# A gated scan kernel: the C rows repacked from DRAM, the gathered rows in another buffer, both outputs ahead of the softplus

## The chip, the cores and the metric

The kernel runs on one core of a Trainium2 chip. The metric is the device time of one execution in microseconds. Five engines are programmed by hand in one file: TensorE (PE in the profile), VectorE (DVE), ScalarE (ACT), GpSimd (POOL) and SyncE (SP), which here only issues transfers. Each has its own instruction stream; they meet only at semaphores. Nothing is scheduled by a tool: the order of an engine's work is the order of the calls in its block.

## What is computed

Sixteen images of 256 channels and 1024 tokens. Group norm and a small mixture of experts give a scale and a shift for each channel; what follows is the second layer:

```python
xz = silu(in_proj_w @ x + in_proj_b)           # 768 x 256
x_ssm, res, gate = split(xz, 3)
xf = silu(conv3(x_ssm, dw_w) + dw_b)           # over tokens, per channel
x_h = gather(xf, perm)                         # a permutation per head, 2 heads
dbc = dbc_w @ xf + dbc_b                       # per head: dt, B (8), C (8)
dt = softplus(dbc[0]); dt, B, C gathered by perm too
h_t = exp(dt_t * A) * h_(t-1) + dt_t * B_t * x_t ;  y_t = C_t . h_t + D * x_t
y = gather(y, inverse of perm)
out = x + silu(out_proj_w @ (y * silu(gate) + res) + out_proj_b)
```

## The kernel before

The work goes in eight **phases** of two images each (`PH`, `NB`). After a prologue (statistics, the ranks that make the permutation, the front half of phase 0) every engine's block calls `cycle(i, ...)` for phase 0, three times a loop of two phases (1 and 2, 3 and 4, 5 and 6), and for phase 7. A cycle does the scan of phase i and, between its parts, the front half (projection, convolution, rows) of phase i + 1.

The permutation goes through DRAM. TensorE turns tiles of `xf` into rows of tokens, ScalarE copies them to `stage` (`rows_out`), VectorE adds a bias, and GpSimd scatters them to `xt_scratch` with 16 indirect transfers (`scatter`, L389). Each row holds the x values of both images and, behind them, dt, B and C. When all have landed, SyncE loads the rows to `xp` in two transfers (`load_rows`, L288: the narrow dt, B, C part, then the wide x part), writes the C part back to `cd_scratch` (`store_c`, L293) and reads it from there into `crow` in 16 transfers that repeat the rows over partitions (`load_c`, L302). The way back is alike: SyncE stores results to `yt_scratch` (L315), and GpSimd gathers them with 8 indirect transfers for each head (`gather`, L401) into `big`; TensorE turns them back (`turn_back`, L1303), VectorE multiplies by the gate (`gated`, L1059).

In chunks of 16 tokens the scan is matrix work. In order: VectorE and ScalarE make the softplus of dt (`softplus`, L958 to L985); TensorE sums it (`segments`, L1214, into `sg`); ScalarE takes eight exponentials (`decays`, L547, into `big`); VectorE makes factors from them (`factors`, L1021 `bblk`); TensorE makes chunk sums (`chunk_sums`, L1230); VectorE scans them (`scans`, L995, semaphore `hs_ready`). GpSimd multiplies the decays by the C rows, 16 instructions for each head (`weigh`, L413, semaphore `w_ready`); VectorE turns these into a causal weight block (`token_weights`, L1038 to L1049, semaphores `m_step`, `mblk_ready`), and TensorE applies it (`results`, L1251 and L1261). GpSimd also scales the projection weights of each image into `wsc` (L358): `weights_x`, `weights_gate`, `weights_residual`. The last is awaited by TensorE's `residual` through `wr_ready`.

TensorE's plain products all stand at L1183: `project`, `gate` and `residual`; the output product is L1313. Their banks `pj0` to `pj3` are drained by ScalarE. Three points of order matter below:

```python
# TensorE, cycle of phase 7 only, ahead of results(i, 0)
if not more:
    residual(i, par, range(0, 4), g_all)      # waits for wr_ready
# ScalarE, end of a cycle
output(i, 0)
if more:
    softplus(i + 1)
output(i, 1)
```

Of the kernel before, what the change touches and what calls it, by code (L numbers as in the profile page):

```python
# [75 lines left out]
def build(nc, x_d, w1g_d, b1g_d, w2_d, b2_d, inw_d, inb_d, dww_d, dwb_d, dbcw_d, dbcb_d, alog_d,  # L76
          dpar_d, mob_d, outw_d, outb_d, const_d, out_d):
    with ExitStack() as ctx:
# [160 lines left out]
        def _(sp):  # L239
# [37 lines left out]

            def load_rows(i):


                sp.wait_ge(rows_scattered, 256 * (i + 1))
# [9 lines left out]
            def store_c(i):  # L291
                sp.wait_ge(dbc_rows_in, 16 * (i + 1))
                sp.dma_start(bass.AP(cd_d, 0, [[S * NB, P], [P * S * NB, H * NT], [1, S * NB]]),  # L293
                             v(xp, NB * (P + 1 + S), (ROW, H * NT), (1, S * NB))).then_inc(c_stored, 16)

            def load_c(i):

                sp.wait_ge(c_stored, 16 * (i + 1))
                run = L * S * NB
# [11 lines left out]
            def cycle(i, par, half, more):  # L311
# [5 lines left out]
                if not last_phase(i):  # L317
                    load_rows(i + 1)
                    store_c(i + 1)
                store_out(i, par, 0)  # L320
                if not last_phase(i):
                    load_c(i + 1)
# [6 lines left out]

            load_rows(0)  # L330
            store_c(0)
            load_c(0)
# [12 lines left out]
        def _(pool):  # L345
# [33 lines left out]
            def scatter(i, tiles):  # L379
                for nt in tiles:  # L380

                    hold(stage_ready, i * NT + nt + 1)
                    if nt == 0:

                        hold(dbc_rows_in, 16 * i)
                        hold(x_rows_in, 16 * i)
                    for h in range(H):
# [5 lines left out]
            def gather(i, h):  # L393
                hold(y_stored[h], 16 * (i + 1))
                if h == 0:

                    hold(mblk_ready, H * (i + 1))
                    hold(hs_ready, H * NB * S * (i + 1))
                for nt in range(NT):
                    k = h * NT + nt  # L400
                    pool.indirect_dma_start(  # L401
                        out=v(big, k * NB * P, (1, NB * P)), out_offset=None, in_=yt_d.ap()[0:(h + 1) * N],
# [16 lines left out]
            def first_tap(i, b):  # L419

                for ot in range(CT):
                    hold(a_drained, i * A_U + b * 4 + ot * 2 + 2)

                    hold(x_full, (i * NB + b) * NT)
                    nc.gpsimd.tensor_scalar(v(xf, ot * N, (1, N)), v(xs, ot * (N + 2), (1, N)), v(small, DWW + ot * 3, (1, 1)), 0.0,  # L425
                                            ALU.mult, ALU.add).then_inc(conv_step[ot], 1)

            def cycle(i, par, half):
                more = not last_phase(i)
                weigh(i, 0)  # L430
                if more:
# [31 lines left out]
        def _(act):  # L463
# [176 lines left out]
            def cycle(i, par, half):  # L640
# [38 lines left out]
                if more:  # L679
                    softplus(i + 1)  # L680
# [766 lines left out]
```

## Time and profile before

| | |
|---|---|
| median of 3 runs | 1151.54 us (1150.46 to 1155.68) |
| profiled execution, its own time | 1155.78 us |
| its span, first to last instruction | 1154.0 us |
| mean granted TensorE clock | 0.853 of 2.4 GHz |
| busy: PE, DVE, ACT, POOL | 850.5, 592.2, 574.9, 531.5 us |

Phase 0's segments begin at 153.7 us, the next ones at 279.4, 407.4, 529.7, 657.8, 787.1, 922.3 and 1049.5 us, so a phase takes 122 to 135 us. No engine is busy all the time. The timeline of one engine lists its instructions, merged where they repeat, with the idle time ahead of them in brackets and what ended it. "remote" there, and "another core or an unknown queue" in the chain, stand for a semaphore event that the profile can't put to an instruction or a transfer; the kernel has one core only. Most numbers below are from phase 4, which stands for 1, 2 and 6 too.

### The profile page before, as it was taken

To read this page: it belongs to the slowest core of one execution; us is meant where nothing else is said; L and a number is where in the kernel's file an instruction comes from. 1 tells how busy PE (TensorE), PEld (TensorE's weight loads), DVE (VectorE), ACT (ScalarE), POOL (GpSimd) and SP (SyncE) were. 2 spreads that over 40 slices of the span, in tenths; PEclk is the share of its full clock that TensorE was granted. 3 is DMA by queue.
4 is the path that set the end of the run, shared out by engine and by line. 5 is a ranking of instruction groups with operands and counts; after the bars stand their busy time and mean duration, and the time that the engine had idled before them with its cause. 6 is when DMAs were issued, how large, how long until landed. Compare 5 with 4: busy or idle time off the path is not lost.

```text
span 1154.0 us, 12950 instructions
## 1 busy us (share of the span) xinstructions
PE 850.5 (74%) x3988; PEld 540.1 (47%) x3988; DVE 592.2 (51%) x1104; ACT 574.9 (50%) x1078; POOL 531.5 (46%) x628
## 2 busy tenths in 40 slices
PE   2039765849984789768995999567984989659946
PEld 0025444624663447534672457334662448425633
DVE  6966138416860468234860587034850578135823
ACT  4824425428652485427552765326552575328541
POOL 0002519560957055642756186623757066723450
PEclk9558767979996799978995999878996899869977
DMA  8830291238524391358032761448024581447132
GB/s 338 329 129 1 77 160 42 89 105 169 136 80 134 105 217 37 115 159 195 31 112 94 179 150 56 134 127 189 32 82 137 145 172 42 141 133 145 39 98 85
DMA packets 112051, 142.54 MB, mean 124 GB/s; under 512 B 41705, under 2 KB 91122, under 8 KB 111986
## 3 DMA queue, kind: packets, MB, share of 16 engines
q1 hardware_dynamic: 99698, 105.91, 35.2%
q0 software_dynamic: 12288, 35.80, 9.5%
q8 instruction: 36, 0.59, 0.2%
q14 instruction: 29, 0.24, 0.1%
HBM read 88.07 MB, written 53.61 MB: 123 GB/s over the span
## 4 chain that ended last, share of the span: by engine, by line
PE 44%; issue 14%; another core or an unknown queue 13%; DMA 9%; DVE 8%; ACT 7%; SPq 3%; POOL 1%; POOLq 0%; ACTq 0%; DVEq 0%
PE pj L1183 17%; DMA xb<-in_x 6%; PE pj L1313 5%; PE pj L1251 4%; PE st L1230 4%; SPq L302 3%; PE tp L1206 3%; PE pj L1261 2%; PE tp L1204 2%; PE tp L1303 2%; ACT big L547 2%; DVE rs L771 1%; PE tp L1241 1%; PE tp L1242 1%
## 5 line engine op out<-in xcount | busy, mean ns | idle before, releaser
L1183 PE MATMUL pj<-xb,wsc 128*128 128x512 f32 x768 | 390.0, 654 | 19.2 <-DMA xb<-in_x 9.6
L413 POOL TENSOR_TENSOR big<-big,crow 128x128 f32<-128x128 f32 x256 | 194.0, 797 | 279.4 <-DMA crow<-cd_scratch 195.6
L1183 PEld LDWEIGHTS pj<-xb,wsc 128*128 128x128 f32 x768 | 151.6, 208 | 180.5 <-issue 172.2
L389 POOL DMA_INDIRECT xt_scratch<-stage,idx x128 | 125.1, 977 | 71.1 <-issue 36.0
L401 POOL DMA_INDIRECT big<-yt_scratch,idx x128 | 124.7, 975 | 65.9 <-issue 37.1
L358 POOL TENSOR_SCALAR wsc<-inw,pcur 128x256 f32<-128x256 f32 x96 | 70.2, 749 | 173.9 <-DVE pcur L916 87.8
L1303 PE MATMUL tp<-cst,big 128*128 128x128 f32 x256 | 48.1, 335 | 131.5 <-DVE gt L1059 65.7
L1059 DVE TENSOR_TENSOR gt<-tp,gt 128x512 f32<-128x512 f32 x64 | 42.3, 688 | 156.6 <-remote 94.0
L559 ACT COPY stage<-tp 128x256 f32<-128x256 f32 x128 | 47.8, 375 | 142.5 <-PE tp L1206 62.6
L1313 PE MATMUL pj<-gt,outw 128*128 128x512 f32 x256 | 112.3, 597 | 0.1
L1303 PEld LDWEIGHTS tp<-cst,big 128*128 128x128 f32 x256 | 36.0, 170 | 152.9 <-DVE gt L1059 69.9
L618 ACT ACTIVATE rs<-pj,pcur 128x512 f32<-128x512 f32 x56 | 36.5, 692 | 136.5 <-PE pj L1183 88.4
L941 DVE TENSOR_TENSOR stage<-stage,small 128x68 f32<-128x68 f32 x64 | 14.7, 230 | 173.4 <-ACT stage L560 107.6
L933 DVE SCALAR_TENSOR_TENSOR xf<-xs,small,xf 128x1024 f32<-128x1024 f32 x64 | 86.2, 1357 | 3.2 <-POOL xf L425 1.4
L1230 PE MATMUL st<-bblk,xp 128*128 128x64 f32 x512 | 68.3, 292 | 21.2 <-DVE bblk L1021 20.3
L1230 PEld LDWEIGHTS st<-bblk,xp 128*128 128x128 f32 x512 | 67.6, 210 | 34.7 <-issue 33.6
L1204 PE MATMUL tp<-cst,xf 128*128 128x128 f32 x256 | 57.1, 308 | 33.3 <-ACT stage L560 20.4
L995 DVE TENSOR_TENSOR_SCAN hs<-big,st 128x64 f32<-128x64 f32 x256 | 49.0, 265 | 63.4 <-PE st L1230 63.4
L1251 PE MATMUL pj<-xp,mblk 128*128 128x128 f32 x512 | 69.6, 280 | 14.6 <-DVE mblk L1049 14.6
L1313 PEld LDWEIGHTS pj<-gt,outw 128*128 128x128 f32 x256 | 48.4, 192 | 58.4 <-issue 58.0
L1206 PEld LDWEIGHTS tp<-dbcw,xf 128*128 128x128 f32 x512 | 73.8, 208 | 0.0
L547 ACT ACTIVATE big<-sg,small 128x400 f32<-128x400 f32 x128 | 63.9, 610 | 19.9 <-POOL big L413 17.2
(192 smaller groups left out, 1317.1 us busy)
## 6 DMA issues: line engine op xcount, KB each, us to landing
xb<-in_x SPq DMA_DIRECT2D x32, 1024.0 KB, 8.0
xp<-xt_scratch SPq DMA_DIRECT2D x8, 2048.0 KB, 9.8
crow<-cd_scratch SPq DMA_DIRECT2D x128, 128.0 KB, 7.9
yt_scratch<-rs SPq DMA_DIRECT2D x16, 1024.0 KB, 4.4
out<-xb SPq DMA_DIRECT2D x16, 1024.0 KB, 4.9
xp<-xt_scratch SPq DMA_DIRECT2D x8, 272.0 KB, 3.5
xt_scratch<-stage,idx POOLq DMA_INDIRECT x128
big<-yt_scratch,idx POOLq DMA_INDIRECT x128
```

The costliest lines, as they stand in the source:

```text
L389: pool.indirect_dma_start(out=xt_d.ap(), out_offset=bass.IndirectOffsetOnAxis(ap=idx[:, k:k + 1], axis=0), in_=v(stage, (nt * H + h) * ROW ...
L401: pool.indirect_dma_start(out=v(big, k * NB * P, (1, NB * P)), out_offset=None, in_=yt_d.ap()[0:(h + 1) * N], in_offset=bass.IndirectOffse ...
L413: last = nc.gpsimd.tensor_tensor(v(big, W_OFF + (s * Q + b * NT) * L, (L, NT), (1, L)), v(big, s * EEW + SEG + b * NT * L, (L, NT), (1, L) ...
L547: last = nc.scalar.activation(v(big, s * EEW, (1, EEW)), v(sg, 0, (1, EEW)), ACT.Exp, scale=v(small, ANEG + h * S + s, (1, 1)))
L933: nc.vector.scalar_tensor_tensor(dst, tap(k), wt(k), dst, ALU.mult, ALU.add).then_inc(conv_step[ot], 1)
L1183: last = nc.tensor.matmul(o[:, :], v(wsc, (b * CT + ct) * 2 * C + slot * C + ot * P, (1, P)), x_view(par, b, ct, nt * HALF, HALF), start=( ...
L1204: nc.tensor.transpose(v(o, ct * P, (1, P)), tile(ct), const("ident"))
L1206: last = nc.tensor.matmul(v(o, 2 * P, (1, H * K1)), tile(ct), v(dbcw, ct * H * K1, (1, H * K1)), start=(ct == 0), stop=(ct == CT - 1))
L1230: last = nc.tensor.matmul(v(st, g * CPT * S, (1, CPT * S)), x_rows(h, b, g), v(bblk, (b * NT + g) * CPT * S, (1, CPT * S)), start=True, st ...
L1251: nc.tensor.matmul(v(pj[2 * b + e], gp * P, (1, P)), v(mblk, (b * NT + g) * P, (1, P)), x_rows(h, b, g), start=(gp == 0), stop=False, skip ...
L1303: last = nc.tensor.transpose(v(o, e * P, (1, P)), v(big, (h * NT + nq * 4 + e) * NB * P + b * P, (1, P)), const("ident"))
L1313: last = nc.tensor.matmul(o[:, :], v(outw, h * C + ot * P, (1, P)), v(gt, (b * CT + h) * N + nt * HALF, (1, HALF)), start=(h == 0), stop=( ...
```

## The change

Six edits that go together:

- **C rows.** `store_c` reads the C part out of `xt_scratch` itself, DRAM to DRAM, ahead of the row load, instead of from `xp` behind it. It now waits for the scatter.
- **Gathered rows** go to `crow` instead of `big`. So `gather` waits for `w_ready` (both weighings of the phase done) instead of `mblk_ready` and `hs_ready`; `load_c` waits until all rows are turned back; `decays` of head 0 no longer waits for that.
- **GpSimd's order**: `weights_residual` behind the second weighing, the first gather ahead of `weights_gate` of the second image.
- **First tap** of the second image's convolution from GpSimd to VectorE.
- **ScalarE's order**: both outputs ahead of the softplus, whose table is loaded once (a set with exponential and logarithm) ahead of its wait; the second image's convolution output behind two more drains.
- **TensorE's order**: two gate products ahead of the wait for `r_ready`.

```diff
+            def store_c(i):
+                sp.wait_ge(rows_scattered, 256 * (i + 1))
+                sp.dma_start(bass.AP(cd_d, 0, [[S * NB, P], [P * S * NB, H * NT], [1, S * NB]]),
+                             bass.AP(xt_d, NB * (P + 1 + S), [[ROW, P], [P * ROW, H * NT], [1, S * NB]])).then_inc(c_stored, 16)
...
-            def load_c(i):
+            def load_c(i, turned):
                 sp.wait_ge(c_stored, 16 * (i + 1))
+                wait(sp, y_full, turned)
...
                 if not last_phase(i):
+                    store_c(i + 1)
                     load_rows(i + 1)
-                    store_c(i + 1)
                 store_out(i, par, 0)
                 if not last_phase(i):
-                    load_c(i + 1)
+                    load_c(i + 1, i * Y_U + Y_U)
...
-                    hold(mblk_ready, H * (i + 1))
-                    hold(hs_ready, H * NB * S * (i + 1))
+                    hold(w_ready, H * (i + 1))
...
-                        out=v(big, k * NB * P, (1, NB * P)), out_offset=None, in_=yt_d.ap()[0:(h + 1) * N],
+                        out=v(crow, k * NB * P, (1, NB * P)), out_offset=None, in_=yt_d.ap()[0:(h + 1) * N],
...
+                weigh(i, 1)
                 weights_residual(i, par)
-                weigh(i, 1)
                 if more:
                     weights_gate(i + 1, 1 - par, 0)
+                gather(i, 0)
+                if more:
                     weights_gate(i + 1, 1 - par, 1)
-                    first_tap(i + 1, 1)
-                gather(i, 0)
...
+                nc.scalar.preload_act_table_set("natural_log_exp_and_others")
                 act.wait_ge(sp_v, i * 9 + 1)
...
                 output(i, 0)
+                output(i, 1)
                 if more:
                     softplus(i + 1)
-                output(i, 1)
...
+                if not first(i):
+                    gate(i, par, range(0, 2), before_g)
                 pe.wait_ge(r_ready, i * 2 + 2)
                 segments(i, 0)
```

Three places show the order of instructions; a row names line, operation, what is written and read, and the semaphores waited for. First GpSimd in a phase inside the loop, from the second weighing to the first scatter, before:

```order
L413 TENSOR_TENSOR big<-big,crow 128x128 x15
L352 ISA
L358 TENSOR_SCALAR wsc<-inw,pcur 128x256 [waits a_full]
L358 TENSOR_SCALAR wsc<-inw,pcur 128x256
L352 REGISTER_ALU
L358 TENSOR_SCALAR wsc<-inw,pcur 128x256 [waits a_full]
L358 TENSOR_SCALAR wsc<-inw,pcur 128x256
L352 REGISTER_ALU
L352 ISA [waits a_drained]
L425 TENSOR_SCALAR xf<-xs,small 128x1024 [waits x_full]
L425 TENSOR_SCALAR xf<-xs,small 128x1024 [waits a_drained,x_full]
```

The first gather followed behind these, with waits for `y_stored0`, `mblk_ready` and `hs_ready`. The same place now:

```order
L413 TENSOR_TENSOR big<-big,crow 128x128 x15
L358 TENSOR_SCALAR wsc<-inw,pcur 128x256 [waits e_full]
L358 TENSOR_SCALAR wsc<-inw,pcur 128x256 x3
L352 ISA
L358 TENSOR_SCALAR wsc<-inw,pcur 128x256 [waits a_full]
L358 TENSOR_SCALAR wsc<-inw,pcur 128x256
L352 REGISTER_ALU
L352 REGISTER_ALU [waits y_stored0]
L401 DMA crow<-yt_scratch,idx 128x256 [waits w_ready]
L401 DMA crow<-yt_scratch,idx 128x256 x7
```

The gather moved ahead of the second image's gate weights and the first taps are gone; the four residual weights stand behind the weighing. Second, GpSimd in phase 7, before:

```order
L413 TENSOR_TENSOR big<-big,crow 128x128 [waits ee_ready,crow_in0,m_step]
L413 TENSOR_TENSOR big<-big,crow 128x128 x15
L358 TENSOR_SCALAR wsc<-inw,pcur 128x256 [waits e_full]
L358 TENSOR_SCALAR wsc<-inw,pcur 128x256 x3
L413 TENSOR_TENSOR big<-big,crow 128x128 [waits ee_ready,crow_in1,m_step]
```

and now:

```order
L413 TENSOR_TENSOR big<-big,crow 128x128 [waits ee_ready,crow_in0,m_step]
L413 TENSOR_TENSOR big<-big,crow 128x128 x15
L413 TENSOR_TENSOR big<-big,crow 128x128 [waits ee_ready,crow_in1,m_step]
L413 TENSOR_TENSOR big<-big,crow 128x128 x15
L358 TENSOR_SCALAR wsc<-inw,pcur 128x256 [waits e_full]
L358 TENSOR_SCALAR wsc<-inw,pcur 128x256 x3
```

The four residual weights moved behind the whole second weighing. Third, ScalarE from the output of phase i to the decays of phase i + 1, before:

```order
L637 ACTIVATE rs<-pj,small 128x512 [waits o_full] x3
L531 ISA
L532 ACT_TABLE_LOAD
L532 ACTIVATE dts<-dts 128x32 [waits sp_v]
L533 REGISTER_ALU
L534 ACT_TABLE_LOAD
L534 ACTIVATE dts<-dts 128x32 [waits sp_v]
L632 REGISTER_ALU
L637 ACT_TABLE_LOAD [waits o_full]
L637 ACTIVATE rs<-pj,small 128x512 [waits z_ready]
L637 ACTIVATE rs<-pj,small 128x512 [waits o_full] x3
L547 ACT_TABLE_LOAD [waits y_full]
```

and now (the output is L623, the softplus L523 and L525, the decays L533):

```order
L623 ACTIVATE rs<-pj,small 128x512 [waits o_full] x3
L521 ACT_TABLE_LOAD
L522 ISA
L523 ACTIVATE dts<-dts 128x32 [waits sp_v]
L524 REGISTER_ALU
L525 ACTIVATE dts<-dts 128x32 [waits sp_v]
L210 ISA [waits w_ready,sg_full]
L533 ACTIVATE big<-sg,small 128x400 [waits hs_ready]
```

Four table loads have become one, and the softplus stands behind all eight output drains.

## Rows read from the trace of the kernel before

**Rows 1.** The page: busy time, chain by engine, costliest groups, transfers to landing.

```profile
PE 850.5 (74%) x3988; PEld 540.1 (47%) x3988; DVE 592.2 (51%) x1104; ACT 574.9 (50%) x1078; POOL 531.5 (46%) x628
...
PE 44%; issue 14%; another core or an unknown queue 13%; DMA 9%; DVE 8%; ACT 7%; SPq 3%; POOL 1%; POOLq 0%; ACTq 0%; DVEq 0%
...
L413 POOL TENSOR_TENSOR big<-big,crow 128x128 f32<-128x128 f32 x256 | 194.0, 797 | 279.4 <-DMA crow<-cd_scratch 195.6
...
yt_scratch<-rs SPq DMA_DIRECT2D x16, 1024.0 KB, 4.4
```

**Rows 2.** Instructions by line and form: busy us, mean ns, idle before.

```profile
L637 ACT ACTIVATE rs<-pj,small 128x512 f32<-128x512 f32 x64 | 40.0, 683 | 31.1 <-PE pj L1313 31.0
...
L547 ACT ACT_TABLE_LOAD x15 | 19.2, 1283 | 9.7 <-issue 9.4 <-PE sg L1216 0.2
...
L929 DVE TENSOR_SCALAR xf<-xs,small 128x1024 f32<-128x1024 f32 x16 | 15.7, 980 | 7.9 <-ACT xs L519 7.9
```

**Rows 3.** Timeline of ScalarE, end of phase 3 and start of 4.

```profile
651.84 1.28 ACT L532 ACT_TABLE_LOAD   x1
...
658.83 1.28 ACT L547 ACT_TABLE_LOAD   x1
660.12 3.99 ACT L547 ACTIVATE big<-sg,small 128x400 f32<-128x400 f32 x8
```

**Rows 4.** Timeline of TensorE, the same stretch.

```profile
644.06 13.90 PE L1313 MATMUL pj<-gt,outw 128*128 128x512 f32 x32
657.79 0.59 PE L1214 MATMUL sg<-rseg,cst 128*128 128x256 f32 x2
...
666.16 1.97 PE L1230 MATMUL st<-bblk,xp 128*128 128x64 f32 x16 [0.45 <-DVE bblk L1021]
...
680.51 8.82 PE L1183 MATMUL pj<-xb,wsc 128*128 128x512 f32 x16 [2.36 <-DMA xb<-in_x]
```

**Rows 5.** Timeline of TensorE in phase 3, chunk sums and projection.

```profile
542.99 3.65 PE L1230 MATMUL st<-bblk,xp 128*128 128x64 f32 x16 [5.43 <-DVE bblk L1021]
...
558.68 3.60 PE L1183 MATMUL pj<-xb,wsc 128*128 128x512 f32 x8
```

**Rows 6.** Timeline of GpSimd, phase 4.

```profile
666.83 7.87 POOL L413 TENSOR_TENSOR big<-big,crow 128x128 f32<-128x128 f32 x16 [26.77 <-DMA crow<-cd_scratch]
...
698.49 3.05 POOL L358 TENSOR_SCALAR wsc<-inw,pcur 128x256 f32<-128x256 f32 x2
...
714.90 1.25 POOL L401 DMA_INDIRECT big<-yt_scratch,idx  x1 [0.87 <-DVE hs L995]
...
724.00 0.95 POOL L401 DMA_INDIRECT big<-yt_scratch,idx  x1 [0.31 <-issue]
...
728.18 0.99 POOL L389 DMA_INDIRECT xt_scratch<-stage,idx  x1 [3.23 <-DVE stage L941]
```

**Rows 7.** Timeline of SyncE's transfers, phases 3 and 4.

```profile
653.67 8.60 SPq L302 DMA_DIRECT2D crow<-cd_scratch  x16
...
699.48 0.37 SPq L315 DMA_DIRECT2D yt_scratch<-rs  x1
```

**Rows 8.** Timeline of VectorE and ScalarE while GpSimd issues gathers, phase 4.

```profile
714.00 5.10 DVE L933 SCALAR_TENSOR_TENSOR xf<-xs,small,xf 128x1024 f32<-128x1024 f32 x4
...
724.97 1.07 ACT L580 COPY rs<-pj 128x512 f32<-128x512 f32 x2 [4.14 <-remote]
```

**Rows 9.** Timeline of ScalarE in the prologue, GpSimd issuing scatters alone.

```profile
137.73 0.69 ACT L597 ACTIVATE gt<-pj,pcur 128x512 f32<-128x512 f32 x1 [1.03 <-issue]
```

**Rows 10.** Timeline of all engines, phase 7.

```profile
1066.40 3.88 POOL L358 TENSOR_SCALAR wsc<-inw,pcur 128x256 f32<-128x256 f32 x4
...
1070.33 4.88 PE L1183 MATMUL pj<-xb,wsc 128*128 128x512 f32 x10 [0.46 <-POOL wsc L358]
...
1073.47 10.88 POOL L413 TENSOR_TENSOR big<-big,crow 128x128 f32<-128x128 f32 x16 [3.19 <-DVE m L1043]
```

**Rows 11.** Timeline of GpSimd, phase 0.

```profile
168.40 7.66 POOL L413 TENSOR_TENSOR big<-big,crow 128x128 f32<-128x128 f32 x16 [23.47 <-DMA crow<-cd_scratch]
```

More of the change, by code:

```diff
@@ L276, in _ @@
                     load_x(i % PH, i % 2, b)
+            def store_c(i):
+                sp.wait_ge(rows_scattered, 256 * (i + 1))
+                sp.dma_start(bass.AP(cd_d, 0, [[S * NB, P], [P * S * NB, H * NT], [1, S * NB]]),
+                             bass.AP(xt_d, NB * (P + 1 + S), [[ROW, P], [P * ROW, H * NT], [1, S * NB]])).then_inc(c_stored, 16)
             def load_rows(i):
-                sp.wait_ge(rows_scattered, 256 * (i + 1))
                 if first(i):
@@ L289, in load_rows @@
                                  bass.AP(xt_d, off, [[ROW, P], [P * ROW, H * NT], [1, width]])).then_inc(loaded, 16)
[L291 to L294, printed above, removed]
-            def load_c(i):
+            def load_c(i, turned):
                 sp.wait_ge(c_stored, 16 * (i + 1))
+                wait(sp, y_full, turned)
                 run = L * S * NB
@@ L328, in cycle @@
                         load_x(i + 2, par, b)
+            store_c(0)
             load_rows(0)
-            store_c(0)
-            load_c(0)
+            load_c(0, 0)
             cycle(0, 0, 0, True)
@@ L386, in scatter @@
                         hold(x_rows_in, 16 * i)
+                        hold(c_stored, 16 * i)
                     for h in range(H):
@@ L417, in weigh @@
                 last.then_inc(w_ready, 1)
[L419 to L426, printed above, removed]
             def cycle(i, par, half):
@@ L453, in _ @@
                 weights_gate(0, 0, b)
-            first_tap(0, 1)
             hold(ranks_ready, 1)
@@ L538, in decays @@
                 act.wait_ge(sg_full, i * H + h + 1)
-                if h == 0:
-                    wait(act, y_full, i * Y_U)
-                else:
-                    act.wait_ge(w_ready, i * H + h)
-                    act.wait_ge(hs_ready, (i * H + h) * NB * S)
+                wait(act, w_ready, i * H + h)
+                wait(act, hs_ready, (i * H + h) * NB * S)
                 for s in range(S):
@@ L666, in cycle @@
                 result(i, 1, 0)
+                turned(i, 1, range(4 + AHEAD, 8))
                 if more:
                     convolved(i + 1, 1)
-                turned(i, 1, range(4 + AHEAD, 8))
                 result(i, 1, 1)
@@ L924, in convolve @@
                     wt = lambda k: v(small, DWW + ot * 3 + k, (1, 1))
-                    if b == 0:
-                        dve.wait_ge(a_drained, i * A_U + ot * 2 + 2)
-                        wait(dve, x_full, i * X_U)
-                        nc.vector.tensor_scalar(dst, tap(0), wt(0), None, ALU.mult).then_inc(conv_step[ot], 1)
+                    dve.wait_ge(a_drained, i * A_U + b * 4 + ot * 2 + 2)
+                    wait(dve, x_full, i * X_U + b * NT)
+                    nc.vector.tensor_scalar(dst, tap(0), wt(0), None, ALU.mult).then_inc(conv_step[ot], 1)
                     for k in (1, 2):
@@ L1302, in turn_back @@
                     for e in range(4):
-                        last = nc.tensor.transpose(v(o, e * P, (1, P)), v(big, (h * NT + nq * 4 + e) * NB * P + b * P, (1, P)), const("ident"))
+                        last = nc.tensor.transpose(v(o, e * P, (1, P)), v(crow, (h * NT + nq * 4 + e) * NB * P + b * P, (1, P)), const("ident"))
                     last.then_inc(y_full, 1)
@@ L1330, in cycle @@
                 else:
-                    gate(i, par, range(0, 4), before_g)
+                    gate(i, par, range(2, 4), before_g)
                     chunk_sums(i, 0, 0)
```

## The prediction

> **What bounds the kernel now.** I read the page's busy line first: no engine is busy three quarters of the time, TensorE comes nearest with 74% [rows 1]. So the chain that ended last: 44% is TensorE, 14% is issue, 13% goes to events the profile cannot name, 9% to transfers [rows 1]. GpSimd carries only 1% of that chain, though a weighing idles 195.6 us in all for the C rows [rows 1]; what GpSimd does matters only where somebody stands waiting for it. Third, the timelines of one phase, engine by engine. In phase 4 ScalarE's end of phase 3 feeds TensorE's sums, VectorE's factors and TensorE's chunk sums, and then TensorE works on to the x projection at 680.51, where it waits 2.36 us for the x rows of the next phase [rows 3, 4]. Behind the results stand y store, gather and turning back. Phase 7 has no next phase to fill gaps, and there TensorE waits straight for GpSimd's residual weights [rows 10]. The granted clock averages 0.853; after an idle stretch TensorE's matmuls run visibly longer.
>
> Four places decide, then. The sum is made against the profiled execution, 1155.78 us (span 1154.0), 4.2 us above the median of 1151.54; I carry differences over to the median unchanged.
>
> **A. Both outputs ahead of the softplus.** Before, the table loads begin at 651.84, between the two outputs, and the segments start at 657.79, right behind the output product (644.06 + 13.90 = 657.96) [rows 3, 4]. That is 5.95 us from the first load to TensorE's sums, hidden under the output product. Now ScalarE drains all eight banks first. The last one ends at 657.96 + 0.68 = 658.65 (683 ns a drain [rows 2]). From there the same path runs, one load of 1.28 shorter [rows 2]: 658.65 + 5.95 - 1.28 = 663.3. Segments are 5.5 us late. The decays started 660.12 - 657.79 = 2.33 us after the segments, of which 1.28 was a load that is now gone, so they start at 664.4 instead of 660.12: 4.3 us late. The chunk sums follow by as much, 670.5 instead of 666.16. TensorE's work from there to the x projection took 680.51 - 2.36 - 666.16 = 12.0 us [rows 4], which gives 682.5 instead of 680.51: the wait of 2.36 us for x soaks up the rest. So +2.0 us. TensorE has waited some 5 us by then instead of 0.45. In phase 3, after a wait of 5.43 us, the chunk sums took 3.65 instead of 1.97 us and the same stretch 558.68 - 542.99 = 15.7 us [rows 4, 5]; with that the projection would be at 686.2, +5.7. The two gate products put ahead of the segments fill part of the wait, so I take the near end, **+2.5 us, bounds +1 (the gate products shorten the stretch) to +5.7, in phases 1, 2, 4 and 6**. In phases 3 and 5, the first of a loop body, that wait of 5 us is already there, before the decays; the late softplus runs under it: **+0.5 each**. Phase 7's share is counted with the last phase.
>
> The loads saved beside that path are worth nothing more. ScalarE is busy half the time [rows 1], and the two on the path are in the sum.
>
> The Trainium skill, "ScalarE: Activation LUTs", section "What ACT_TABLE_LOAD costs", would price a switch at about 2.66 us, 1283 ns of load and some 1380 ns to drain the engine. The rows have the load, and the next instruction 1.29 us behind its start (658.83 to 660.12) [rows 3], so no drain shows and the trace does not agree. By the page's figure A would be about 1.4 us less for each load taken off the path.
>
> **B. The first gather earlier, the first tap on VectorE.** The gather began at 714.90, behind a wait for scans [rows 6]. Now it needs the y store (699.48 + 4.4 = 703.9 [rows 7, 1]) and a free GpSimd: second weighing done at 698.49, four residual weights by phase 7's row 3.88, two gate weights 3.05 [rows 6, 10], so 705.4. It starts some 10 us earlier, and nothing is waiting for that: the scatter behind it is bound by `stage` (3.23 us at 728.18), not by GpSimd [rows 6].
>
> What the gather does to others counts. From the sixth of eight gathers (714.90 to 724.00, one each 1.30 us) until after the last, ScalarE stood 4.14 us at 724.97 for an event the trace calls remote, although the products it copies were long done [rows 6, 8]. In the prologue, where GpSimd issues scatters alone, such a wait is 1.03 us [rows 9]. I take it that signals for ScalarE and VectorE come late while gathers are being issued. Moved, the gather clears 724.97 (-4.14) but lays the late stretch over 711 to 716, where the convolution's drains and the scans depend on TensorE's signals; as one such event was 4.14, and not every one there is on the path, I put +3 there. The first tap of image 1 goes to VectorE, two instructions of 980 ns [rows 2]: +2.0, ahead of the other taps (5.10 us at 714.00 [rows 8]). The gate weights of image 1 behind the gather have cover until the next drains. The rest of the waits gains some 1.4 us from the stage coming earlier. **B = -4.14 + 3 + 2 - 1.4 = -0.5 us for each of phases 0 to 6.** Its bounds: nothing late in the new place, -4.14 + 2 - 1.4 = -3.5; a full 4.14 there twice over, +4.
>
> The gathered rows in `crow` add a wait of `load_c` for all turning back. That ended before the output product begins at 644.06, while the loads of `crow` are issued at 653.67 behind `out` stores [rows 4, 7]. It costs nothing in phases 1 to 7; without that cover it would push the 26.77 us wait of the first weighing [rows 6]. For the same reason reading C from DRAM sooner gains nothing there: 653.67 is set by stores queued ahead.
>
> **C. Phase 0.** No output stands ahead of `load_c`, so C rows written before the wide row load do arrive sooner; the first weighing, which waited 23.47 us for `crow` until 168.40 [rows 11], starts earlier, but the dt rows land later by the store ahead of them. **-1.5 us**, bounds -4 and +2.
>
> **D. The last phase.** TensorE's residual product waits for the four residual weights: GpSimd made them from 1066.40 to 1070.28, TensorE began at 1070.33 [rows 10]. Now they stand behind the second weighing. That waits for VectorE's `m` anyway (3.19 us) and ran 1073.47 to 1084.35; the weights add 3.88: 1088.2. The product starts 18 us late. In TensorE's order all results of the phase stand behind it, behind those y store, gather, turning, output. Nothing later has slack: TensorE waited only on itself. Add 2 us, phase 7's A, which moves the second weighing too, and 1.4 us for a slower start after so long an idle (8.82 us for 16 matmuls after 2.36 us idle in phase 4 [rows 4], where this phase's 16 took about 7.4). **+21 us**, bounds +18 and +25. In the loop phases TensorE's residual product is behind the results, and the later weights are hidden.
>
> **Sum:** C -1.5, A 4 x 2.5 + 2 x 0.5 = +11, B 7 x -0.5 = -3.5, D +21: +27. Profiled 1182.8; median **1178.5 us**.
>
> **Rivals.** A measurement of this kernel can tell about 0.5%, 5.8 us, from no change: 1145.8 to 1157.3.
> - *The new place of the gather is quiet.* B = -3.5 in seven phases: -1.5 + 11 - 24.5 + 21 = +6.0, 1157.5 us, at the edge of what can be told from no change. For it: I infer the late signals from a few waits. Against: the gathers' issue is the same, and there is TensorE work to be signalled at 711 too. Chance 0.14.
> - *Faster: the phase's tail shrinks.* The most these rows allow is delay and stage wait together, 4.14 + 3.23 = 7.4 us a phase, if scatters and the second gather move up as well: -1.5 + 11 - 51.8 + 21 = -21.3, 1130.2 us. It decides below zero from B = -4.4, below 1145.8 from -5.2. For it: the second gather follows the scatter at once. Against: `stage` comes from ScalarE behind the convolution, which the extra tap delays. Chance 0.13.
> - *Low clock and late signals add up.* A = +5.7, B = +1: -1.5 + 22.8 + 1 + 7 + 23 = +52, 1204 us. For it: a 5 us wait did cost that in phase 3 [rows 5]. Chance 0.12.
> - *The edit in phase 7 costs less than it says*, because something else ends last there: D = +6 gives 1163.5 us. The row names GpSimd as releaser with 0.46 us [rows 10], so 0.04.
> - *GpSimd's issue is stopped by VectorE.* The moved gather runs under VectorE's two-input work of up to 5.10 us a stretch [rows 8]. Were descriptors held for that long, B = -0.5 + 5.1 = +4.6: +27 + 36 = +63, 1214 us. Against: with these taps running from 714.00 on, the eight gathers kept 1.30 us apart [rows 6, 8]. Chance 0.02. It is the rule of the Trainium skill, "SBUF — State Buffer", section "🔬 SBUF: two separate sides", where VectorE holding the shared port pair blocks GpSimd's descriptor writes; the trace does not show it.
>
> **The numbers.** My forecast has 0.55, its own range 1167 to 1191 (A between +1 and +4, B between -2 and +1, D from 18 to 25). Faster 0.15 (the tail case, the edge of the quiet one), same 0.11 (most of the quiet case), slower 0.74. The range 1149 to 1195 leaves out the tail case and the two heavy ones.
>
> **What the changed profile would show.** D: TensorE's first residual product in phase 7 waits about 18 us for `wsc`, and its end is that much later from its segments than before. A: ScalarE's eight drains unbroken, one table load, segments 4 to 6 us behind the output product; the wait for x nearly gone. B: gathers from some 16 us after the first results instead of 26, ScalarE's remote wait moved ahead of them; the results-to-output stretch within 2 us of before. C: first weighing earlier than 168.4. Wrong would be the forecast if that stretch shrinks by over 5 us a phase, or if TensorE in phase 7 does not stand.

## The result, and the profile after

The changed kernel takes 1192.08 us (median of 4 runs, 1180.3 to 1193.0), the kernel before 1153.61 us beside it (4 runs, 1150.46 to 1162.62). The ratio is 1.0297, with a 95% interval of 1.0209 to 1.0385: 3% slower. A ratio here and below is estimated from the single undisturbed runs and need not be the quotient of the two medians. By the ratio the change costs 34 us, by the medians 38.5, where 27 were forecast. The profiled execution took 1193.0 us, with a span of 1190.8. The page of the changed kernel, busy time, chain and the weighing's group:

```profile
PE 859.5 (72%) x3988; PEld 552.0 (46%) x3988; DVE 606.1 (51%) x1120; ACT 547.8 (46%) x1055; POOL 540.0 (45%) x612
...
PE 49%; issue 18%; DVE 13%; another core or an unknown queue 9%; ACT 7%; POOL 2%; DMA 1%; SPq 0%; DVEq 0%; POOLq 0%; ACTq 0%
...
L413 POOL TENSOR_TENSOR big<-big,crow 128x128 f32<-128x128 f32 x256 | 203.3, 831 | 324.7 <-ACT big L533 275.7 <-DVE m L1028 29.9 <-DMA crow<-cd_scratch 19.1
```

Against [rows 1], ScalarE is 27 us less busy (the loads saved), transfers fell from 9% of the chain to 1%, and the weighing waits for C rows 19.1 us instead of 195.6. Yet the weighing idles longer in all, now for ScalarE's decays (275.7 us), and DVE and issue took the transfers' share of the chain. In the loop phases the C rows do not come sooner: their loads are issued 4.1 to 4.4 us ahead of the output product's end in both traces. In phase 4 the decays end 10.6 us behind that end instead of 6.2, so that they, and not the rows, are what the weighing now waits for.

Four points in TensorE's timeline cut each phase into stretches: the segments, the first results, the start and the end of the output product. In us, for two pairs of traces of before and after. The second pair comes from another chip, number 4 (runs e5 and e6 below):

| stretch | before | after | before, chip 4 | after, chip 4 |
|---|---|---|---|---|
| C: phase 0, segments to results | 31.6 | 26.6 | 31.0 | 26.9 |
| A: phases 1 to 6, end of output product to results, sum | 196.8 | 224.9 | 194.5 | 215.0 |
| B: phases 0 to 6, results to output product, sum | 570.2 | 560.5 | 564.9 | 567.1 |
| D: phase 7, end of output product to results | 28.0 | 54.2 | 27.9 | 50.8 |
| D: phase 7, results to the end of its output product | 70.0 | 66.4 | 69.0 | 65.4 |

In the first pair A gives +28.1, B -9.7, D +22.6, and C -4.3 (its segments began 0.7 later): +36.7, and the spans differ by 36.8 us. In the second pair A gives +20.5, B +2.2, D +19.3 and C -1.7: +40.3; the output products are 1.0 us shorter in all, and the spans differ by 39.3 us.

The timeline of ScalarE in the changed kernel, end of phase 3 and start of 4, where [rows 3] stood before:

```profile
671.13 0.69 ACT L623 ACTIVATE rs<-pj,small 128x512 f32<-128x512 f32 x1 [1.03 <-PE pj L1298]
671.84 1.28 ACT L521 ACT_TABLE_LOAD   x1
673.13 0.23 ACT L523 ACTIVATE dts<-dts 128x32 f32<-128x32 f32 x1
...
677.73 3.98 ACT L533 ACTIVATE big<-sg,small 128x400 f32<-128x400 f32 x8 [3.89 <-PE sg L1201]
```

The same stretch of TensorE:

```profile
657.20 13.90 PE L1298 MATMUL pj<-gt,outw 128*128 128x512 f32 x32
670.93 3.60 PE L1168 MATMUL pj<-xb,wsc 128*128 128x512 f32 x8
676.47 0.70 PE L1199 MATMUL sg<-rseg,cst 128*128 128x256 f32 x2 [1.94 <-DVE rtot L970]
...
684.09 3.64 PE L1215 MATMUL st<-bblk,xp 128*128 128x64 f32 x16 [3.04 <-DVE bblk L1006]
...
704.90 3.70 PE L1168 MATMUL pj<-xb,wsc 128*128 128x512 f32 x8 [0.77 <-ACT gt L583]
```

One load stands where four did. But it comes behind the last drain, and the segments start 676.47 - 671.10 = 5.4 us behind the output product's end, in every phase from 1 to 7 alike, where they had started at once [rows 4]. In phase 4 TensorE now idles twice, 1.94 and 3.04 us. The chunk sums then take 3.64 us instead of 1.97. The wait of 2.36 us for x rows is gone, with 0.77 us for a drain in its place.

How much the clock costs in phase 4 shows between two traces of this same kernel. TensorE's chunk sums of phase 4 in the trace from chip 4:

```profile
686.52 1.97 PE L1215 MATMUL st<-bblk,xp 128*128 128x64 f32 x16 [1.64 <-DVE bblk L1006]
```

and the table of stretches (us, busy time of each engine, granted clock, DMA share, GB/s) of the changed kernel, first chip, from its chunk sums to the gate products behind them:

```profile
684.10:694.90 10.80, 10.80 (x43) 8.55 (x43) 2.83 (x9) 4.15 (x6) 8.77 (x17) 0.56 0.97 282
```

and of the same work on chip 4:

```profile
686.50:692.70 6.20, 6.18 (x42) 5.19 (x43) 2.88 (x9) 4.18 (x6) 6.20 (x12) 1.00 1.07 286
```

The same 42 or 43 matmuls take 10.80 us at a granted clock of 0.56, nearly all of it the 1.2 GHz level, and 6.20 at 1.00. From end of output product to results that phase takes 37.3 us in the one and 33.0 in the other; before it took 31.2 and 29.7. So A cost 6.1 us there on the first chip and 3.3 on chip 4. The 4.3 us between the two traces of the changed kernel are not all A's: the kernel before also ran slower on the first chip, its projection in 8.82 us instead of 7.13. Over the six stretches of A, TensorE's busy time for the same matmuls rose from 171.9 to 186.1 us in the first pair and from 168.9 to 180.2 in the second. So 14.2 of 28.1 us, and 11.3 of 20.5, are matmuls that took longer; the rest is idle time. The granted clock over this stretch of phase 4 fell from 0.95 to 0.86, on chip 4 from 1.00 to 0.95.

GpSimd in phase 4 of the changed kernel, where [rows 6] stood:

```profile
682.22 9.74 POOL L413 TENSOR_TENSOR big<-big,crow 128x128 f32<-128x128 f32 x16 [40.64 <-ACT big L533]
...
724.98 1.02 POOL L401 DMA_INDIRECT crow<-yt_scratch,idx  x1 [0.16 <-issue]
...
727.57 2.53 POOL L401 DMA_INDIRECT crow<-yt_scratch,idx  x1 [0.30 <-issue]
...
736.45 1.02 POOL L401 DMA_INDIRECT crow<-yt_scratch,idx  x1 [0.30 <-issue]
...
744.67 1.03 POOL L390 DMA_INDIRECT xt_scratch<-stage,idx  x1 [4.17 <-issue]
```

The gather starts 16.5 us behind the first results (708.44) instead of 25.7, as worked out. It wins little: GpSimd then stands 4.17 us for the stage, and the scatter starts 36.2 us behind the first results instead of 39.0. And ScalarE's remote waits of that phase, of which the first was 4.14 us at 724.97 [rows 8], stand later:

```profile
763.03 0.37 ACT L545 COPY stage<-tp 128x256 f32<-128x256 f32 x1 [7.35 <-remote]
...
771.45 0.37 ACT L545 COPY stage<-tp 128x256 f32<-128x256 f32 x1 [7.95 <-remote]
```

Over both engines the remote waits sum to 223 us before and 212 after, on chip 4 to 196 and 224: moved, not removed. In phase 7 alone they shrink, from one wait of 6.55 us to 1.53, on chip 4 from 6.58 to 2.23.

Phase 7 of the changed kernel, GpSimd:

```profile
1095.94 10.82 POOL L413 TENSOR_TENSOR big<-big,crow 128x128 f32<-128x128 f32 x16 [11.58 <-DVE m L1028]
1106.74 1.83 POOL L358 TENSOR_SCALAR wsc<-inw,pcur 128x256 f32<-128x256 f32 x4
```

and TensorE:

```profile
1108.63 9.51 PE L1168 MATMUL pj<-xb,wsc 128*128 128x512 f32 x16 [15.21 <-POOL wsc L358]
```

Against [rows 10], everything up to the chunk sums is done, TensorE stands 15.21 us for four small instructions that wait behind a weighing, and the product then needs 9.51 us instead of 7.46. And the first weighing of phase 0:

```profile
163.65 7.64 POOL L413 TENSOR_TENSOR big<-big,crow 128x128 f32<-128x128 f32 x16 [19.10 <-DMA crow<-cd_scratch]
```

It starts 4.75 us earlier than in [rows 11].

### The profile page after: what moved, and what is told of

Read it like the earlier page. It is cut to its first block, busy times and chain, and to the rows that moved or that the text cites. A ratio compares the mean times of both kernels' runs of the same rounds, so it can differ in the third digit from the quotient of the medians.

```text
span 1190.8 us, 12917 instructions
## 1 busy us (share of the span) xinstructions
PE 859.5 (72%) x3988; PEld 552.0 (46%) x3988; DVE 606.1 (51%) x1120; ACT 547.8 (46%) x1055; POOL 540.0 (45%) x612
## 4 chain that ended last, share of the span: by engine, by line
PE 49%; issue 18%; DVE 13%; another core or an unknown queue 9%; ACT 7%; POOL 2%; DMA 1%; SPq 0%; DVEq 0%; POOLq 0%; ACTq 0%
PE pj L1168 17%; PE pj L1298 9%; PE st L1215 6%; ACT big L533 3%; PE tp L1191 3%; PE pj L1236 3%; PE tp L1189 2%; PE tp L1288 2%; PE pj L1246 2%; DVE xf L918 1%; DVE rs L757 1%; DVE m L1025 1%; PE tp L1227 1%; DVE bblk L1006 1%
## 5 line engine op out<-in xcount | busy, mean ns | idle before, releaser
L413 POOL TENSOR_TENSOR big<-big,crow 128x128 f32<-128x128 f32 x256 | 203.3, 831 | 324.7 <-ACT big L533 275.7
L401 POOL DMA_INDIRECT crow<-yt_scratch,idx x128 | 141.6, 1106 | 72.0 <-issue 37.6
L1288 PE MATMUL tp<-cst,crow 128*128 128x128 f32 x256 | 48.8, 339 | 146.5 <-DVE gt L1044 81.1
L1288 PEld LDWEIGHTS tp<-cst,crow 128*128 128x128 f32 x256 | 36.5, 172 | 167.5 <-DVE gt L1044 83.8
L1215 PE MATMUL st<-bblk,xp 128*128 128x64 f32 x512 | 74.6, 309 | 32.7 <-DVE bblk L1006 31.8
L1215 PEld LDWEIGHTS st<-bblk,xp 128*128 128x128 f32 x512 | 74.1, 227 | 48.2 <-issue 47.1
L604 ACT ACTIVATE rs<-pj,pcur 128x512 f32<-128x512 f32 x56 | 36.7, 691 | 123.9 <-PE pj L1168 71.2
L533 ACT ACTIVATE big<-sg,small 128x400 f32<-128x400 f32 x128 | 63.7, 609 | 50.1 <-PE sg L1201 23.9
L556 ACT COPY ch<-tp 128x256 f32<-128x256 f32 x128 | 42.4, 381 | 70.3 <-PE tp L1227 58.6
```

The lines of the kernel that those rows point to most:

```text
L401: pool.indirect_dma_start(out=v(crow, k * NB * P, (1, NB * P)), out_offset=None, in_=yt_d.ap()[0:(h + 1) * N], in_offset=bass.IndirectOffs ...
L413: last = nc.gpsimd.tensor_tensor(v(big, W_OFF + (s * Q + b * NT) * L, (L, NT), (1, L)), v(big, s * EEW + SEG + b * NT * L, (L, NT), (1, L) ...
L533: last = nc.scalar.activation(v(big, s * EEW, (1, EEW)), v(sg, 0, (1, EEW)), ACT.Exp, scale=v(small, ANEG + h * S + s, (1, 1)))
L1215: last = nc.tensor.matmul(v(st, g * CPT * S, (1, CPT * S)), x_rows(h, b, g), v(bblk, (b * NT + g) * CPT * S, (1, CPT * S)), start=True, st ...
L1288: last = nc.tensor.transpose(v(o, e * P, (1, P)), v(crow, (h * NT + nq * 4 + e) * NB * P + b * P, (1, P)), const("ident"))
```

## The experiments

The first four ran together on one chip, number 12. Their reference came out at 1066 us, not 1153; the fifth and the sixth were made to find out why. A ratio is always to the kernel before on the same chip.

**e1, the residual weights of phase 7 early.** One place of the changed kernel, in GpSimd's cycle (`i` is the phase, `more` is false in phase 7 only):

```diff
-                weigh(i, 1)
-                weights_residual(i, par)
+                if not more:
+                    weights_residual(i, par)
+                weigh(i, 1)
+                if more:
+                    weights_residual(i, par)
```

> The changed kernel, with the four residual weights of phase 7 ahead of the second weighing again (the other phases stay changed). Theory: TensorE's wait of 15.21 us for wsc in phase 7 goes, and with it the slow start behind it (16 matmuls in 9.51 us); 1192 - 20 = 1172 us, and segments to results of phase 7 near 31 us instead of 48.9. Rival: something else in phase 7 is as late, and less than 8 us come back (over 1184 us).

Measured: 1058.47 us against 1066.0, ratio 0.9946 (0.9916 to 0.9976). The ratio's interval stands in brackets, here and below. The wait for `wsc` is a third of what it was; TensorE in phase 7 of e1:

```profile
974.65 9.28 PE L1171 MATMUL pj<-xb,wsc 128*128 128x512 f32 x16 [5.40 <-POOL wsc L358]
```

What is left of the change is 0.5% faster on this chip than the kernel before. The 1172 us could not be tested here.

**e2, the softplus between the outputs.** The changed kernel with

```diff
                 output(i, 0)
-                output(i, 1)
                 if more:
                     softplus(i + 1)
+                output(i, 1)
```

> The changed kernel, with the softplus between the two outputs again (its preload and TensorE's two early gate products stay). Theory, from the stretches of the changed kernel's trace: the late softplus costs 27 us in phases 1 to 6 and a few in phase 7; 1192 - 30 = 1162 us, with segments 13.7 us behind the start of the output product instead of 19.3 and no half-speed chunk sums in the phases 1, 2, 4 and 6. Rival, the prediction's own size: 11 us, so 1181 us, since behind the softplus the x rows or the C rows are as late again.

Measured: 1087.32 us, ratio 1.0201 (1.013 to 1.0271).

**e3, both.**

> Both of these undone. Theory: the costs add, 1192 - 20 - 30 = 1142 us, which is faster than the kernel before by 1%: the rest of the change (C rows from DRAM, gathered rows in crow, earlier gather, first tap on VectorE) is worth -9.5 us in the results-to-output stretches and -4 us in phase 0. Rival: the gain in those stretches came only from transfers and clock being rested by the longer idle ahead, and is lost with it: 1150 to 1156 us, as before.

Measured: 1070.54 us, ratio 1.0045 (1.0014 to 1.0077). From e3 to e2 is D, 17 us. From e1 to e3 the softplus's place: putting it back between the outputs costs 12 us here, the other sign than A. Both theories on it fall for this chip. In e3 the stretches ahead of the results of phases 1 to 6 sum to 268.0 us, in e1 to 249.4. ScalarE in e3, phase 5:

```profile
731.60 0.23 ACT L526 ACTIVATE dts<-dts 128x32 f32<-128x32 f32 x1 [9.54 <-DVE dts L946]
```

and TensorE there:

```profile
734.36 5.33 PE L1171 MATMUL pj<-xb,wsc 128*128 128x512 f32 x8 [7.45 <-ACT rs L626]
```

ScalarE stands 9.54 us for dt rows that have not landed, with four drains queued behind it; TensorE's two early gate products need the banks of these drains, 7.45 us, and the segments stand behind them. So e3 is not a clean "without A": it keeps the gate products' new place, which goes badly with the old place of the softplus. On the page this is one group, 52.0 us of waits:

```profile
L1171 PE MATMUL pj<-xb,wsc 128*128 128x512 f32 x768 | 388.1, 649 | 65.0 <-ACT rs L626 52.0
```

**e4, gate products twice.** The changed kernel with the idle stretch ahead of the chunk sums filled, in TensorE's `gate`:

```diff
+                    if not first(i) and k in (2, 3):
+                        part(o, par, b, 0, k // 2 % 2, k % 2)
                     part(o, par, b, 0, k // 2 % 2, k % 2).then_inc(g_full, 1)
```

> The changed kernel, with TensorE computing the gate products 2 and 3 of phases 1 to 7 twice over (same banks, same result; 8 extra matmuls, 3.6 us a phase), in the place where it waited 3 us for the chunk factors. Theory: half of the late softplus's cost is the clock at half for some 10 us behind the idle stretch; with that stretch filled the chunk sums run in 1.97 instead of 3.64 us, the granted clock there stays near 1, and despite 25 us more of TensorE work the time falls by 7 x 2 = 14 us, to 1178 us. Rival: the clock falls anyway, or costs nothing on the path: the work adds 0.5 to 3.6 us a phase, 1195 to 1215 us.

Measured: 1071.5 us, ratio 1.0019 (0.9981 to 1.0057). TensorE in phase 4 of e4:

```profile
605.70 7.80 PE L1168 MATMUL pj<-xb,wsc 128*128 128x512 f32 x16
613.34 1.89 PE L1215 MATMUL st<-bblk,xp 128*128 128x64 f32 x16
```

and of e1, which differs from it in this stretch by the filling alone:

```profile
606.86 5.29 PE L1171 MATMUL pj<-xb,wsc 128*128 128x512 f32 x8
613.18 1.97 PE L1218 MATMUL st<-bblk,xp 128*128 128x64 f32 x16 [1.02 <-DVE bblk L1009]
```

Sixteen matmuls cost 2.5 us more than eight and take up the 1.02 us wait. From end of output product to results, phases 1 to 6, e4 sums to 248.1 and e1 to 249.4 us: 22 us of added work in these phases came free. But it bought nothing either, since on this chip the first chunk sums of every phase take 1.97 us without it. Whether it helps where they take 3.64 us stays untested: neither e4 nor e10 came to such a chip.

**e5 and e6, the two kernels again.**

> The changed kernel as it is, on the chip that this call gets. In the last four runs the kernel before took 1066 us where it had taken 1153.6, and the traces show no remote waits (212 to 223 us of them in the two traces of the first chip); results-to-output took 59 us a phase instead of 81. So what the change costs was never measured beside the four edits. Theory: on a chip without late signals the last phase costs the same (17 us, from the ratio 1.0201 of the second run less 1.0045 of the third) and the late softplus nothing, as TensorE waits there for the dt rows anyway: 1.01, some 1076 us at 1066 for before. Rival: it costs 3% here too, 1098 us. If the call gets a chip like the first, 1192 us.

> The kernel before as it is, for its trace on the same chip as the runs beside it. Theory: without remote waits the results-to-output stretches are near 59 us, and TensorE waits 8 to 14 us behind the output product for the next phase's dt rows, 1066 us in all. Rival: the remote waits are still there in the kernel before and were taken away by what all four variants share.

They ran on chip 4, which is like the first. The change: 1189.31 us against 1152.97, ratio 1.0315 (1.0213 to 1.0417), which repeats the result. The kernel before, run once for its trace: 1147.62 us. Both traces show the remote waits (table and sums above). In none of the ten traces from chips 12, 3 and 14 is there one, and e11 below is the kernel before up to phase 7. So the rival on e6, that the variants had removed the waits, falls: on five chips they go with the chip, not with the kernel.

**e7 and e8, e1 and e3 again,** with the same diffs.

> The first experiment once more (only the residual weights of phase 7 ahead of the second weighing again), because chips turned out to differ: on some the kernel before takes about 1153 us and shows some 200 us of remote waits, on another 1066 us and none. Theory, from the stretches of the two pairs of traces of the first kind: 1190 - 20 = 1170 us there, still slower than before by 1.3%, since the late softplus costs 20 to 27 us. On the other kind the first experiment's ratio of 0.995 comes again. Rival: the rest of the change is harmless on any chip, and the ratio is below 1.005.

> The third experiment once more (residual weights of phase 7 early, softplus between the outputs). Theory on a chip of the first kind: 1190 - 20 - 24 = 1146 us, ratio 0.99 to 1.00: what is left is worth the 4 us of phase 0 and at most 9 us in the results-to-output stretches. On the other kind 1.0045 again. Rival: a ratio of 1.015 or more, so that the stretches ahead of the results were not the softplus's doing.

They came to chip 3, one without remote waits: 1056.6 and 1069.47 us against 1063.93, ratios 0.995 (0.9917 to 0.9983) and 1.0035 (1.001 to 1.006). Both repeat chip 12; the claims on the other kind stay untested.

**e9, the gather late.** e3 with, on GpSimd,

```diff
                     weights_gate(i + 1, 1 - par, 0)
-                gather(i, 0)
-                if more:
                     weights_gate(i + 1, 1 - par, 1)
+                gather(i, 0)
```

> As the run beside it with both edits undone, and the first gather of each phase behind the gate weights of the second image again (the first tap stays on VectorE, the gathered rows in crow). The theory of step B says that the gather's early place gives back as much as it costs: within 0.3% of the run beside it on either kind of chip, with remote waits at 725 to 745 us of the trace instead of ahead of them. Rival, the tail case: the early gather is worth 2 to 7 us a phase, and this run is 14 us slower or more.

Measured: 1070.77 us, ratio 1.0054 (1.0029 to 1.0078), against 1069.47 for e8. The early gather is worth 1.3 us by the medians and 0.2% by the ratios, inside the stated 0.3% and not clear of the intervals. The tail case falls on this chip, and there are no remote waits to place.

**e10, e4 again.**

> The fourth experiment once more (the change, with gate products 2 and 3 computed twice where TensorE waits). Theory on a chip of the first kind: the time falls from 1190 to about 1178 us, ratio 1.02 instead of 1.03, because chunk sums at 1.97 instead of 3.64 us and a full clock behind them are worth more than the added work. On the other kind 1.002 again. Rival: 1.033 or more.

Measured: 1071.41 us, ratio 1.0089 (1.0044 to 1.0134), more than the 1.002 expected. In the stretches it stands beside e7 as e4 beside e1 (246.7 to 245.3 us).

**e11, D alone in the kernel before.**

```diff
-                weights_residual(i, par)
+                if more:
+                    weights_residual(i, par)
                 weigh(i, 1)
+                if not more:
+                    weights_residual(i, par)
```

> The kernel before with one edit: in phase 7 the four residual weights stand behind the second weighing. Step D by itself. Theory: 18 us later start of TensorE's residual product and a slower start behind the idle time, +18 to +22 us on a chip of either kind: ratio 1.016 to 1.020. Its trace also shows the other phases of the kernel before on this call's chip. Rival: under 1.010, if the second weighing had also been ahead of something else that now comes sooner.

Measured on chip 14: 1080.0 us against 1062.14, ratio 1.0176 (1.0149 to 1.0204): 18.7 us by the ratio, 17.9 by the medians, and the ratio is inside the stated range. TensorE in its phase 7:

```profile
994.99 9.62 PE L1186 MATMUL pj<-xb,wsc 128*128 128x512 f32 x16 [19.26 <-POOL wsc L358]
```

**e12, A alone in the kernel before:** `output(i, 1)` ahead of `softplus(i + 1)`, the preload, and the gate products 0 and 1 ahead of TensorE's wait for `r_ready`, as in the change's diff. It ran on chip 14 too.

> The kernel before with three edits that go together: both outputs ahead of the softplus, one table preloaded ahead of its wait, and TensorE's first two gate products ahead of the segments. Step A by itself. Theory: its sign depends on the chip. Where the remote waits are (before near 1153 us) the dt rows have long landed and it costs 3 to 4 us a phase: ratio 1.015 to 1.022. Where they are not (before near 1065 us) ScalarE stands for the dt rows with four drains behind it, and moving them ahead gains what the first and third experiment differ by, 10 to 13 us: ratio 0.988 to 0.992, which would beat both kernels. Rival: with C rows still written behind the row load the first weighing is bound by crow, and it changes nothing on either.

Measured: 1063.11 us, ratio 1.0016 (0.9986 to 1.0045): nothing. The gain of 10 to 13 us falls, and what e1 and e3 differ by belongs to their surroundings: the kernel before has no gate product ahead of the segments that could wait for the held drains (argued from the rows of e3, not tried apart). The table of stretches for the chips without remote waits:

| stretch, sums in us | e11, before but for D | e12, A alone | e1 | e7 |
|---|---|---|---|---|
| phases 1 to 6, end of output product to results | 238.0 | 234.8 | 249.4 | 245.3 |
| phases 0 to 6, results to output product | 429.2 | 430.7 | 414.0 | 414.8 |

With the rest of the change (e1, e7) TensorE reaches its output product 2 us a phase sooner, some 15 in all, and gives 7 to 15 of it back behind it. The gather's early place is not what gains: e9, with the gather late, has 411.8 us in the second row. Which of the other edits does was not tried apart. VectorE in e1, phase 5, waits there for rows that come no sooner, 77.1 us behind the first results of phase 4:

```profile
716.65 0.29 DVE L946 SCALAR_TENSOR_TENSOR dts<-xp 128x16 f32<-128x16 f32 x2 [9.31 <-DMA xp<-xt_scratch]
```

and in e11, the kernel before, for the same rows, 74.1 us behind them:

```profile
720.92 0.29 DVE L961 SCALAR_TENSOR_TENSOR dts<-xp 128x16 f32<-128x16 f32 x2 [3.19 <-DMA xp<-xt_scratch]
```

## Why the prediction was right, and where it was not

**Sign and size.** 1178.5 us was forecast with a range to 1195.0, 1192.08 was measured. The sign and the order of size are right, and the wide range of 1149 to 1195 holds it. The main case's own range of 1167 to 1191 is missed by 1 us. The terms did worse than their sum. D was to be the largest, and A came out larger. In the first pair A is 17 us above its value and B 6 below, so that the sum is nearer than A. The measured time lies between the forecast and the 1204 us of the rival "low clock and late signals add up", and the low clock of that rival is what came: A in phases 1, 2, 4 and 6 averages +5.8 us in the first pair, as in that rival, and +3.7 in the second. Its other half, B = +1, did not come in the first pair, and came to +0.3 a phase in the second.

**D, the last phase: the mechanism right, and shown.** The working gave a start 18 us late, 2 us of A and 1.4 us of clock, +21. In the traces the product begins 39.5 us behind the segments instead of 20.8, 18.7 later, and phase 7 as a whole costs 22.6 and 19.3 us in the two pairs. Inside it errors cancel. The weights take 1.83 us, not 3.88, and the second weighing starts 2.9 us later from the segments. Counted from the end of the output product, the residual product starts 24.2 us later, where 18 + 2 were worked out, and the results 26.3. Behind the results the phase is then 3.6 us shorter (3.5 in the second pair), where the working put nothing. ScalarE's remote wait there is 5 us shorter, but the cause was not tried. e11 has D alone at 18.7 us, e3 to e2 at 17.

The 3.88 us was not what the four weights cost by themselves. Three of them took 0.48 or 0.49 us, and one stood under a two-input instruction of VectorE, in phase 7 of the kernel before:

```profile
1066.46 2.56 DVE L1038 TENSOR_TENSOR big<-big,bc 128x2048 f32<-128x2048 f32 x1 [0.65 <-POOL big L413]
...
1066.86 2.51 POOL L358 TENSOR_SCALAR wsc<-inw,pcur 128x256 f32<-128x256 f32 x1
```

All twelve weights of that trace that took over 2 us overlap a two-input TENSOR_TENSOR of VectorE more than any other instruction of it; in the new place in phase 7 none does, and four take 1.83 us.

**A, the softplus: mechanism right, size wrong.** The segments' 5.5 us came out: 5.4 us behind the output product's end in every phase, where they had started 0.2 us ahead of it. The term was the choice of the near end, +2.5, "the two gate products put ahead of the segments fill part of the wait". They don't fill enough: 1.94 and 3.04 us of idle remain, and the far end with chunk sums at low clock, +5.7, is what phase 4 shows, +6.1. Chip 4 has the same lateness without the low clock there, and +3.3. Phase 1, at +7.6 in the first pair, is beyond the far end. In phases 3 and 5, put at +0.5, it cost 4.4 and 0.6 in the first pair, 1.5 and 4.0 in the second: the old wait covers the late softplus in part only. All in all +28.1 and +20.5 us where the sum had 11. That A costs this on chips with remote waits rests on two pairs of traces, and was not tried by itself there. On chips without them A alone costs nothing (e12).

**B, the gather and the tap: small, as forecast.** -3.5 was forecast, -9.7 and +2.2 were measured, on average -1.4 and +0.3 us a phase where -0.5 was put. Single phases differ by -8.2 to +5.2 us, so the agreement is one of the sum. (The upper bound's sum, -4.14 + 8.28 + 2 - 1.4, makes +4.7 and not +4; nothing hangs on it.) Start of the gather, the remote waits moved and not gone, the scatter bound by the stage: all as worked out. The +3 us put where the gather now stands came on one chip: on chip 4 phase 4 has a remote wait of 3.37 us there, and five of the seven phases have 3 us or more. In the first chip's trace phases 1 to 6 have nothing there; the waits behind it grew in phase 4 from about 4.5 to 7.35 and 7.95 us. The quiet case and the tail case both fall. The idea behind them, that late signals come with gathers, needs a correction: chips 12, 3 and 14 issue the same gathers and show none.

**C, phase 0:** -1.5, within its bounds in one pair (2.5 us later segments, 4.1 us shorter stretch: -1.6), a little past them in the other (-4.3). In the later phases the C rows come no sooner, as said, for the stores queued ahead.

**The loads.** The Trainium skill, "ScalarE: Activation LUTs", section "What ACT_TABLE_LOAD costs", adds a drain of some 1380 ns to each load. The changed trace has its first exponential 1.29 us behind the start of the load (671.84 to 673.13), so again no drain shows, as in [rows 3].

**GpSimd's issue under VectorE.** This rival had a chance of 0.02, as the gathers kept 1.30 us apart [rows 6]. In the new place they do not: eight take from 724.98 to 736.45, 1.64 us apart, and one took 2.53 us. VectorE at the same time in the changed kernel:

```profile
726.99 2.29 DVE L1034 TENSOR_TENSOR mblk<-m,cst 128x2048 f32<-128x2048 f32 x1
...
734.04 2.61 DVE L918 SCALAR_TENSOR_TENSOR xf<-xs,small,xf 128x1024 f32<-128x1024 f32 x2
```

The long one (727.57 to 730.10) lies over `mblk`, another of 1.72 us over the taps, both with two inputs. It costs some 2.4 us per gather of eight, hidden under the 4.17 us that the scatter waits. In the whole changed trace 14 of 128 gathers take over 1.4 us, and all lie over `mblk` (8) or the taps (6). But lying there is not enough: in the trace before 26 gathers lie over the taps, and none of them takes so long. The rule of the Trainium skill, "SBUF — State Buffer", section "🔬 SBUF: two separate sides", that such a GpSimd transfer can be held while VectorE has the shared ports, fits this trace better than the trace before; at 0.3 us an issue instead of the 5.1 us a phase that the rival put on it. That the ports are what holds these issues was not tried.

**What stays open.** Why chips differ, and what the remote events are. The change itself was not timed on a chip without remote waits; the ratios of e1 and e11 together make about 1.012 (an estimate), and e4 and e10, the change with the added gate products, measured 1.002 and 1.009. Also open is whether e1's kernel, 0.5% faster than the kernel before on two chips, is faster where the remote waits are. By the table, where D is some 20 us of 36, it would be slower than before there (an estimate, not run).

## What to carry to other kernels

Work behind one engine's queue is priced where somebody waits for it: four instructions of half a microsecond, put behind a weighing of 10.8 us, cost 18.7 us (e11) in the one phase that has nothing else to do. In the seven others TensorE has no wait for them in either trace of the changed kernel. Moving drains ahead of the next phase's first step trades one engine's table loads for a later start of the whole chain, and half of what that cost in the first pair was TensorE at a lower clock behind longer idle stretches. And take the reference on the chip of the experiment, every time: one and the same edit had another sign of effect in another surrounding, and the kernel another bound on another chip.

## What the runs showed of the hardware that was not expected

The five chips fall in two kinds for this kernel. On the first chip and chip 4 the kernel before takes some 1153 us, with about 200 us of remote waits and 81 us from results to output product; on chips 12, 3 and 14 it takes 1062 to 1066 us, with no remote wait and 61 us. There TensorE waits behind the output product for the dt rows instead. The change itself was timed on the first kind alone, and ten of the twelve experiments on the other.
